# Attention: the product of masked scores and values, with its weights taken in two halves of 64 queries

## The reference

```python
q = _phi((x @ W_Q.T).reshape(b, t, H, DK))      # H = 8 heads, DK = 64, phi = elu + 1
k = _phi((x @ W_K.T).reshape(b, t, H, DK))
v = (x @ W_V.T).reshape(b, t, H, DK)
def step(carry, inp):                           # over the tokens
    S = g4 * S + jnp.einsum('bhi,bhj->bhij', kt, vt)
    z = g3 * z + kt
    num = jnp.einsum('bhij,bhi->bhj', S, qt)
    den = jnp.sum(z * qt, axis=-1, keepdims=True) + EPS
    return ((S, z), num / den)
gate = jax.nn.sigmoid(x @ W_g_w.T + W_g_b).reshape(b, t, H, DK)
y = (outputs * gate).reshape(b, t, H * DK)
return y @ W_O.T
```

## Time and profile before

| | |
|---|---|
| median of three runs | 1033.98 us (1030.67 to 1035.63) |
| the profiled execution: its time, its span | 1030.6 us, 1028.8 us |
| PE, PEld busy | 883.3 us (86%), 749.9 us (73%) |
| DVE, ACT, POOL busy | 551.7 us (54%), 449.5 us (44%), 477.5 us (46%) |
| line 595: MATMUL, LDWEIGHTS | 64.2 us and 61.5 us busy, 512 of each, mean 280 and 196 ns |
| idle of DVE before `den` (line 753) until line 595 was done | 36.9 us in 32 waits |

### The profile page before, as it was taken

How to read it: one execution, slowest core, us unless ns; L and a number is a source line. 1 busy time by engine, 2 the same in 40 slices (tenths; PEclk the granted TensorE clock), 3 DMA queues, 4 the chain that set the end, 5 groups by cost and what they waited for, 6 DMA issues and landing times. The chain is left out here.

```text
span 1028.8 us, 24712 instructions
## 1 busy us (share of the span) xinstructions
PE 883.3 (86%) x8764; PEld 749.9 (73%) x8764; DVE 551.7 (54%) x1617; ACT 449.5 (44%) x957; POOL 477.5 (46%) x501
## 2 busy tenths in 40 slices
PE   4999999999999832998667779999986999999991
PEld 2787778777777731877564569999885679999991
DVE  4665666566665543655438958455385822222226
ACT  5535354353544200655327647533323544444444
POOL 3234343533435434677766400015604176767774
PEclk9999999999999875999979999999997999999996
DMA  7778500000000001333250001000005013322245
GB/s 248 256 277 329 208 17 5 21 8 13 13 8 20 22 19 52 103 103 101 60 165 2 2 3 23 3 4 3 1 2 207 11 55 88 94 79 88 87 119 164
DMA packets 72918, 79.28 MB, mean 77 GB/s; under 512 B 14429, under 2 KB 56676, under 8 KB 72320
## 3 DMA queue, kind: packets, MB, share of 16 engines
q1 hardware_dynamic: 61744, 59.69, 18.2%
q0 software_dynamic: 9216, 16.84, 4.8%
q10 hardware_dynamic: 1872, 1.58, 0.5%
HBM read 32.46 MB, written 47.77 MB: 78 GB/s over the span
## 5 line engine op out<-in xcount | busy, mean ns | idle before, releaser
L436 POOL TENSOR_TENSOR attn_qd<-attn_qT,attn_qpow 128x512 f32<-128x512 f32 x32 | 54.5, 1702 | 154.5 <-DVE attn_qT L726 154.5
L1465 ACT ACTIVATE routed_hT<-routed_hid,routed_B 128x256 f32<-128x256 f32 x160 | 65.8, 471 | 81.0 <-PE routed_hid L1388 81.0
L1034 POOL DMA_INDIRECT mixed<-moe_outs,moe_target x80 | 77.8, 972 | 38.4 <-DVE moe_outs L1136 16.2
L1306 POOL DMA_INDIRECT results<-routed_outs,routed_target x80 | 78.5, 981 | 28.3 <-issue 16.6
L1291 POOL DMA_INDIRECT queue_in<-routed_XN,routed_slot x64 | 64.0, 1000 | 47.1 <-DVE routed_slot L1566 22.2
L1400 PE MATMUL routed_outp<-routed_W,routed_hT 128*128 128x128 f32 x640 | 77.8, 275 | 0.0
L1388 PE MATMUL routed_hid<-routed_cols,routed_W 128*128 128x256 f32 x320 | 75.8, 380 | 0.5 <-DVE routed_cols L1614 0.5
L1400 PEld LDWEIGHTS routed_outp<-routed_W,routed_hT 128*128 128x128 f32 x640 | 74.7, 192 | 0.1
L595 PE MATMUL attn_av<-attn_v,attn_a 128*128 128x65 f32 x512 | 64.2, 280 | 9.3 <-DVE attn_a L737 8.9
L595 PEld LDWEIGHTS attn_av<-attn_v,attn_a 128*128 128x128 f32 x512 | 61.5, 196 | 13.4 <-DVE attn_a L737 12.7
L426 POOL DMA_INDIRECT sorted_rows<-attn_sent_rows,attn_slot x56 | 55.9, 998 | 18.3 <-issue 14.3
(11 more groups left out here) (332 smaller groups left out, 2275.2 us busy)
## 6 DMA issues: line engine op xcount, KB each, us to landing
sorted_rows<-attn_vacant SPq DMA_DIRECT2D x8, 2080.0 KB, 7.4
moe_rows<-sorted_rows SPq DMA_DIRECT2D x44, 130.0 KB
queue_in<-attn_empty SPq DMA_DIRECT2D x8, 645.0 KB, 7.1
routed_rows<-queue_in SPq DMA_DIRECT2D x40, 129.0 KB, 2.3
results<-attn_zero SPq DMA_DIRECT2D x8, 512.0 KB, 7.8
ssm_turn_buf<-mixed SPq DMA_DIRECT2D x16, 256.0 KB, 3.7
routed_W<-m1w SPq DMA_DIRECT2D x2, 2048.0 KB, 10.4
xs<-x SPq DMA_DIRECT2D x8, 256.0 KB, 4.4
```

The costliest lines, as they stand in the source:

```text
L436: pool.tensor_tensor(wide(of_pair(qd, p)), wide(of_pair(qT, p)), qpow[:, p * P:(p + 1) * P].unsqueeze(1).to_broadcast([P, BATCH, P]), ALU. ...
L1034: pool.indirect_dma_start(results, bass.IndirectOffsetOnAxis(target[:, n:n + 1], 0), outs[q][:, j * P:(j + 1) * P], None, bounds_check=2 * ...
L1306: pool.indirect_dma_start(results, bass.IndirectOffsetOnAxis(target[:, n:n + 1], 0), outs[t % KEPT_BACK][:, j * P:(j + 1) * P], None, boun ...
L1465: last = act.activation(hT[t % 2][:, m * GROUP:(m + 1) * GROUP], banks[q % 4][:, (m % 2) * GROUP:(m % 2 + 1) * GROUP], ACT.Silu, bias=B1[: ...
```

## The change

`values` issues twice as many products. Each product's weights are cut in two halves of 64 queries (columns of `a`); the output of the first half goes to partitions 0 to 63 of `av`, that of the second to partitions 64 to 127, at the same columns. What is streamed, the value block of 65 columns, is the same for both halves. Waits, sums in `av` and the signal after the last product are as before, and no other function is touched (lines behind it move by two: 604 is 606, 612 is 614).

```diff
                 for b in range(BATCH):
                     for h in range(2):
-                        mm = pe.matmul(av[:, h * 512 + b * (DK + 1):h * 512 + (b + 1) * (DK + 1)],
-                                       a[:, h * WIDE + b * P:h * WIDE + (b + 1) * P], v4[:, b, 2 * p + h, :],
-                                       start=False, stop=True, skip_group_check=True)
+                        for rows in (slice(0, P // 2), slice(P // 2, P)):
+                            first = h * WIDE + b * P
+                            mm = pe.matmul(av[rows, h * 512 + b * (DK + 1):h * 512 + (b + 1) * (DK + 1)],
+                                           a[:, first + rows.start:first + rows.stop], v4[:, b, 2 * p + h, :],
+                                           start=False, stop=True, skip_group_check=True)
                 mm.then_inc(s["av"], 1)
```

## The result

The changed kernel takes 1009.54 us in the median against 1034.81, a ratio of 0.976 (95% interval 0.972 to 0.980). A second measurement gave 1008.95 against 1030.96, 0.978 (0.976 to 0.981). So it is faster by 22 to 25 us; 17 were forecast. One launch of the first series, at 1178.1 us with a granted clock of 0.731, was disturbed: it is left out of the ratio but stands in the median of four, and the other three have a median of 1008.33 us.

The account below looks back on a forecast made before the run. PE, with the loop through `values`, was taken to bound the attention layer. 31 blocks x 0.45 = 14.0 us plus 1.3 for the slow block, 15.3 off 1030.6, gave 1015.3; 1017 was named, range 1009 to 1027.

Parts of the forecast that it names:

- The forecast's own signs: In the changed profile: block 1.25 to 1.4 us, ordinary step 8.4 instead of 8.83, DVE's wait from 36.9 to 22.
- the forecast's best bound: Block of 32 pairs at the 64*64 products' pace, 33 ns a pair: 1.06 us, saving 0.68 a step, 22 us.
- The row of the same form: `new_state` in the trace, 16 pairs of 128*64 with 128x65 streamed in 0.61 us, 38 ns a pair.
- two such blocks are 1.22 us: The new `values` block of 32 pairs costed as twice `new_state`'s 0.61 us, before the form's price.
- The price of changing the form: Going from whole to half arrays on PE costs 0.07 us a block, read from transposes of 0.50 against 0.43.
- A shorter block brings the next one forward by the same amount: In the loop through `values`, PE's and DVE's paths start at the block's end, so all 32 steps count the saving.
- I cost it at nothing, and at most at 0.1 us: `values_gates` waiting for ACT's last Relu behind the block: nothing, at most 0.1 us in seven steps with p = 2.
- the slow block: The one `values` block at the lower clock level: from 3.48 to 2.2 us, 1.3 us saved.
- halves share one resource in turn: Rival: two half loads take as long as one whole, 54.5 ns each, block stays 1.74 us, no change; chance 0.06.
- Taken back in the loop: Rival: steps where PE waits for `a` save nothing, leaving 18 x 0.45 = 8 us, so 1022.5 or 1026; chance 0.06.
- The clock did not fall more often: Rival: more clock falls at p = 0, 1.66 us each, up to 1067; 9 more falls decide; chance 0.04.
- a half costs what a whole does: Rival: a half pair in `values` takes 109 ns, 56 us lost, 1086; chance 0.04.

Follow-up runs that it names:

- two kernels: The changed kernel, ratio 0.976, and the changed kernel with halves only in steps with p = 3 and whole products elsewhere, ratio 0.998.
- the ACT experiment: Changed kernel with ACT making the router's rows after the four Exp and Relu instead of before them at p = 2: 1008.79 us, ratio 0.979.
- quarters: Changed kernel with the values product in four quarters of 32 queries, 1007.40 us, ratio 0.977; with ACT's router rows later too, 1008.30 us, ratio 0.979.
- half the products: Changed kernel with the values product for two of the four batches only, 16 narrow pairs a block instead of 32: 1002.72 us.
- the kernel that does not alternate: Changed kernel with its 32 pairs reordered, first the 16 to partitions 0 to 63, then the 16 to 64 to 127: 1030.22 us, ratio 0.9995.

## Why the prediction was right

The mechanism and the direction were right; that the range held the time is in part luck. In the profile 15.3 us were forecast and 22.3 came: 4.8 more in the 28 steps and 3.0 more in the last chunk, less 0.8 in front of the first block and behind the start of the last. The forecast's own signs missed on the strong side: the block is 1.08 us and not 1.25 to 1.4, the ordinary step 8.32 and not 8.4, DVE's wait 13.2 us and not 22. The block came near the forecast's best bound, 1.06 us.

**The block.** The row of the same form carried the sum, and it was the right one: `new_state` runs narrow pairs in different halves by turns, and so does the new block. The step of the forecast that was mis-sized is "two such blocks are 1.22 us": a block has 0.14 us that does not grow with its pairs, and doubling 0.61 counted it twice. Measured is 1.08, where the forecast had 1.29 with its 0.07. (The forecast calls the entries of `new_state` 448 products; they are 448 pairs, 224 products.)

**The price of changing the form.** 0.07 us was forecast. Measured is 0.10 in front of the block and 0.05 to 0.06 behind, some 0.15 us, visible only outside the block. For a step in which PE sets the pace the two errors partly cancel: 0.51 saved where 0.45 was forecast. Where PE had waited for `a`, the load's exposure was there before already (1.84 us), so the full 0.74 comes back, and that made the mean of a loop step 0.59.

**The loop.** "A shorter block brings the next one forward by the same amount" held on PE's own path and behind p = 3 (8.92 us in two kernels). It did not hold where an engine has work of its own in front of what it does for the block: behind p = 1 DVE lets 0.14 us of 0.75 go, and "I cost it at nothing, and at most at 0.1 us" failed. PE waits for the first Relu too, which the forecast had not looked at, and with the form's price the step behind p = 2 keeps 0.32 us; the ACT experiment adds 0.3 to that.

**28 steps** were to save 28 x 0.45 = 12.6 us and saved 17.4, of which about 1.6 are a fall of the clock that the kernel before does not always have. That leaves 15.8, 0.56 a step, where 0.45 was forecast.

**The last chunk** saved 5.2 us where 2.2 was forecast (1.3 for the slow block and 0.45 for each of the other two). Three things make it up. The block at the lower level was costed alone, but the whole way behind it changed: 358.88 - 350.09 = 8.79 us before, 336.71 - 330.10 = 6.61 after, 2.2 us. The clock's second fall at p = 0 is missing: 13.56 against 11.29 us, of which 0.7 is the shorter block, so 1.5 us. The step behind p = 1 gave 0.74. PE at the place of the slow block now, beside the earlier trace rows:

```profile
330.10 1.56 PE L597 MATMUL attn_av<-attn_v,attn_a 128*64 128x65 f32 x32 [3.10 <-DVE attn_a L739]
331.58 1.12 PE L561 MATMUL attn_turn<-attn_ident,attn_xr 128*128 128x128 f32 x4
...
336.71 1.15 PE L597 MATMUL attn_av<-attn_v,attn_a 128*64 128x65 f32 x32
```

In both kernels the clock falls at the end of PE's pause of over 3 us or just behind it. Before, the granted clock is 0.50 in the whole block and 0.62 up to the next one; after, 0.68 in the block of 1.48 us and 0.74 up to the next one. The way there is 8.3 to 10.1 us in the profiles whose block with p = 2 is as long as before or longer, 6.4 to 6.6 in the three with halves, and 5.1 and 6.6 in quarters; in the 5.1 the clock did not fall at all. With half the products it is 7.2, so it does not simply follow the block's length. Why the clock falls later or comes back earlier was only observed.

**The rivals.** That halves share one resource in turn was refuted: 34 ns a pair over the block, 29 without the fixed part, below 54.5. The rule cited for it, from the Trainium skill, page "TensorE: Matmul & The Clock Gate", section LDWEIGHTS (loading the stationary operand), gives 53 ns for 64 columns and 107 for 128, estimates from the page. This agrees with the kernel that does not alternate (57 ns a pair) and with the whole products (109 ns), not with neighbours in different halves. "Taken back in the loop" happened in part in two of the four kinds of step, behind p = 1 and p = 2. The clock did not fall more often. That a half costs what a whole does was refuted by the same 34 ns.

## What to carry to other kernels

Where few columns are streamed (65) through wide weights (128), the load set PE's pace; cutting the weights' columns into halves that go to different output partitions, one half right after the other, made the block 1.6 times as fast. It gains nothing when the halves are not neighbours in program order, or when as many columns are streamed as are loaded, and quarters add almost nothing to halves once streaming fills each part. When a block of a known form is scaled up, take two sizes of it and separate the fixed part; and follow each engine's wait behind the shortened block, for its first part too and not only for the last.

## What the runs showed of the hardware

- Four quarters of the array take float32 pairs at 16.4 ns each, 64 in a row, behind a wait or not. MATMULs for different quarters start 7 ns apart, so taking in instructions was not the limit at that pace.
- Of an instruction on DVE and one on POOL that ran side by side, the one that began second took longer. In steps with p = 2 of the changed kernel the features of keys (128x512) took 1.68 us when they began just after POOL's `qd` (170.70 against 170.56; `qd` took 1.28). In the step before they began just ahead of it (161.19 against 161.24) and took 0.64, and `qd` 1.72. With ACT's later order the features came first again and took 0.64. It cost nothing here: the scores behind began 0.53 us after the transposes with and without it, and `y` was still in time.
